# The adaptive norm's first shift and scale made ahead of the other ten, in a two-layer transformer kernel on one Trainium2 core

## The chip, the cores and the metric

The kernel runs on one core of a Trainium2 chip. The metric is the device time in microseconds (us) of one execution. The engines are named as in the profile: PE is the matrix engine (TensorE), PEld its loads of weights, DVE is VectorE, ACT is ScalarE, POOL is GpSimd, SP is SyncE, which here only issues transfers (DMAs). Each engine has a program of its own, runs it in order, and waits on semaphores that other engines and transfers raise.

## What is computed

Two layers act on x (8 sequences, 256 tokens, 128 features). In each, a conditioning vector c gives twelve 128-wide vectors per sequence in all, six a layer, which shift, scale and gate.

```
mod = (silu(c) @ wmod).reshape(8, 6, 1, -1)          # once for each layer, c: 8x128, wmod: 128x768
sa, ca, ga, sb, cb, gb = mod[:, 0], ..., mod[:, 5]
ga, gb = (2*(g >= 0) - 1) * max(abs(g), 0.25)        # for each gate g
h = layernorm(x) * (1 + ca) + sa
x = x + ga * attention(h)                            # layer 0: gated delta rule; layer 1: chunked state space
h = layernorm(x) * (1 + cb) + sb
x = x + gb * ffn(h)                                  # layer 0: 8 experts, top 2; layer 1: butterfly maps
```

The attention of layer 0 projects h to q, k, v and two gates, convolves over four tokens, takes norms, and runs a recurrence over time.

## The kernel before

Features lie on the partitions, tokens along the free axis. The 256 tokens are cut into five windows (32, 32, 64, 64, 64 tokens of each sequence) that pass through the stages of layer 0 behind each other, and into four views of 64 tokens for layer 1. What each engine does, in which order, is written out by hand at the end of its part of `program`, as a list of calls such as `center(("front", 0))` or `project(0, i)`. The function names differ by engine, and the work of one stage is spread over several of them.

The first window's prologue is the part that matters here. SP's `loads` issues the transfers in a fixed order on one queue: x of window 0, the constants C (256 KB), the conditioning vectors `csil` (8 KB), the modulation weights `wm` (768 KB; their space is the upper buffer of `wrep`, by which name the profile knows them), the columns of biases `col` (31.5 KB), the projection matrices M (576 KB), the x of the other windows, then the operands of a fold of the butterfly maps (`wxT` in `ssdb`, `wc`, and a ring of eight 256 KB pieces `hid`), and more. A semaphore rises by 16 for each transfer that has landed.

The layer norm of a window is made in pieces: PE takes the mean away (`center`, psA), ACT squares (`ln_square`), PE averages the squares (`variance`, psB), ACT makes 1/sqrt with a Ln and an Exp (`ln_scale`), DVE multiplies (`ln`, into hf), ACT applies scale and shift, one instruction for each sequence (`modulate`). Then PE projects (`project`) and ACT applies silu to the projections (`projected`).

The modulation: ACT applies silu to both conditioning vectors (`condition`), PE makes twelve products of 128x128 weights with eight columns (`modulation`, psM bank X0, a float32 product being two passes, so 24 passes), DVE copies all to `mod`, adds one to the scales and makes the gates (`modulation`, eight instructions). ACT's `table` loads a new table of functions where the next function isn't in the one held. The silu, the Ln and Exp, and the square root each need a table of their own here.

In the prologue the orders before are: on ACT `ln_square`, `condition`, `ln_scale`, `modulate`, `projected`; on PE `center`, `variance`, `modulation`, `project`, then `fold(0)` and `square_sums(0)` (the sums for the norms of keys and queries); on DVE `biases`, `modulation`, `ln`, `convolve`. On SP the ring's later loads (`fold_load`) wait for folds.

## Time and profile before

| | |
|---|---|
| median of 3 runs | 572.57 us (570.67 to 573.45) |
| the profiled execution | 571.0 us |
| its span, first to last instruction | 568.9 us |
| mean granted TensorE clock | 0.904 of full speed |
| busy: PE, DVE, ACT, POOL | 78%, 66%, 69%, 34% |

The span is what the rows' times count from; 2.1 us of the profiled execution lie outside it. In the timeline's rows the first number is the start, the second the time that the merged instructions cover, "x24" how many there were, and the brackets tell how long the engine was idle before and what ended that. The weight loads (PEld) overlap with the passes (PE).

### The profile page before, as it was taken

To read this page: it belongs to the slowest core of one execution; us is meant where nothing else is said; L and a number is where in the kernel's file an instruction comes from. 1 tells how busy PE (TensorE), PEld (TensorE's weight loads), DVE (VectorE), ACT (ScalarE), POOL (GpSimd) and SP (SyncE) were. 2 spreads that over 40 slices of the span, in tenths; PEclk is the share of its full clock that TensorE was granted. 3 is DMA by queue.
4 is the path that set the end of the run, shared out by engine and by line. 5 is a ranking of instruction groups with operands and counts; after the bars stand their busy time and mean duration, and the time that the engine had idled before them with its cause. 6 is when DMAs were issued, how large, how long until landed. Compare 5 with 4: busy or idle time off the path is not lost.

```text
span 568.9 us, 6438 instructions
## 1 busy us (share of the span) xinstructions
PE 445.5 (78%) x2064; PEld 303.8 (53%) x2064; DVE 376.6 (66%) x663; ACT 392.6 (69%) x661; POOL 193.0 (34%) x188
## 2 busy tenths in 40 slices
PE   5585597479975777998969989999999889864145
PEld 4474573267654654665746656676656566441012
DVE  1326958698979999799998958999231483022800
ACT  3798747757898558689745997746996676924242
POOL 0150961396108971048791104541003000030001
PEclk9988777978999999899988998999999999985557
DMA  7637537232270311800240081000000000000000
GB/s 204 231 122 180 164 100 300 47 93 75 67 140 1 93 40 56 188 0 1 60 109 0 1 189 38 1 1 1 0 1 20 1 1 1 0 18 0 1 1 18
DMA packets 35473, 36.49 MB, mean 64 GB/s; under 512 B 12904, under 2 KB 30832, under 8 KB 35184
## 3 DMA queue, kind: packets, MB, share of 16 engines
q1 hardware_dynamic: 35152, 31.88, 21.2%
q10 hardware_dynamic: 288, 4.19, 1.9%
q8 instruction: 17, 0.28, 0.2%
q14 instruction: 16, 0.13, 0.1%
HBM read 31.61 MB, written 3.28 MB: 61 GB/s over the span
## 4 chain that ended last, share of the span: by engine, by line
PE 34%; DVE 22%; ACT 16%; POOL 11%; issue 9%; DMA 2%; SPq 2%; POOLq 0%; DVEq 0%; ACTq 0%
PE psF L751 8%; PE psS L769 8%; PE psB L708 4%; DVE XX L1798 3%; DVE norm L1795 3%; DVE U L1815 3%; DVE T L1813 3%; DVE T L1817 3%; PE psM L812 3%; ACT L1086 2%; ACT hid L1280 2%; ACT L1088 2%; ACT hS L1129 2%; PE psM L819 2%; POOL G L2154 2%
## 5 line engine op out<-in xcount | busy, mean ns | idle before, releaser
L769 PEld LDWEIGHTS psS<-we2s,hid 128*128 128x128 f32 x1024 | 136.5, 196 | 61.2 <-issue 46.9
L751 PE MATMUL psF<-h,we1s 128*128 128x512 f32 (+1 forms) x320 | 139.7, 528 | 13.2 <-ACT hid L1280 12.5
L769 PE MATMUL psS<-we2s,hid 128*128 128x128 f32 x1024 | 138.9, 280 | 10.8 <-DVE acc L1836 5.5
L1280 ACT ACTIVATE hid<-psF,col 128x512 f32<-128x512 f32 (+1 forms) x160 | 93.2, 598 | 57.6 <-PE psF L751 56.9
L2203 POOL TENSOR_TENSOR QS<-H,qn 128x512 f32<-128x512 f32 x32 | 44.8, 1414 | 95.3 <-DVE H L1823 86.0
L751 PEld LDWEIGHTS psF<-h,we1s 128*128 128x128 f32 x320 | 54.9, 199 | 41.5 <-ACT hid L1280 22.0
L1836 DVE SCALAR_TENSOR_TENSOR acc<-psS,gate,acc 128x128 f32<-128x128 f32 x128 | 36.3, 340 | 33.7 <-PE psS L769 33.7
L1823 DVE TENSOR_TENSOR_SCAN H<-A,T 128x576 f32<-128x576 f32 x32 | 55.3, 1727 | 1.1
L1088 ACT ACT_TABLE_LOAD x41 | 52.6, 1283 | 0.7
L1813 DVE TENSOR_TENSOR T<-wrep,H 128x648 f32<-128x648 f32 x32 | 33.6, 1050 | 14.3 <-DMA wrep<-XX 13.9
L1815 DVE TENSOR_REDUCE U<-T 128x64 f32<-128x576 f32 x32 | 38.7, 1208 | 1.1
L1086 ACT ACT_TABLE_LOAD x30 | 38.5, 1283 | 0.5
L708 PE MATMUL psB<-QS,worep 128*128 128x256 f32 x128 | 32.1, 408 | 7.5 <-POOL QS L2203 7.0
L2225 POOL TENSOR_TENSOR x<-x,brS 128x512 f32<-128x512 f32 x4 | 5.8, 1462 | 93.8 <-DVE brS L1971 93.8
L590 PE MATMUL psA<-x,C 128*128 128x512 f32 (+3 forms) x36 | 21.2, 677 | 16.1 <-DMA C<-consts_dram 6.1
L2186 POOL TENSOR_TENSOR zb<-bg,kn 128x192 f32<-128x192 f32 (+10 forms) x35 | 32.4, 959 | 0.4
L708 PEld LDWEIGHTS psB<-QS,worep 128*128 128x128 f32 x128 | 25.7, 205 | 12.1 <-POOL QS L2203 7.6
L1766 DVE SCALAR_TENSOR_TENSOR zb<-p,col,zb 128x512 f32<-128x512 f32 (+1 forms) x45 | 25.5, 640 | 9.5 <-ACT zb L1184 9.5
L1817 DVE TENSOR_TENSOR T<-krep,U 128x512 f32<-128x512 f32 x32 | 30.7, 959 | 1.1
L2229 POOL TENSOR_TENSOR brS<-brS,mod 128x512 f32<-128x512 f32 x4 | 4.3, 1081 | 77.2 <-ACT brS L1322 77.2
L1106 ACT ACTIVATE sq<-psA 128x512 f32<-128x512 f32 (+3 forms) x18 | 9.8, 544 | 28.3 <-PE psA L590 28.3
L2154 POOL TENSOR_TENSOR G<-G,ag 128x64 f32<-128x64 f32 (+10 forms) x35 | 28.4, 810 | 2.4
(193 smaller groups left out, 734.7 us busy)
## 6 DMA issues: line engine op xcount, KB each, us to landing
wrep<-scratch_dram SPq DMA_DIRECT2D x64, 144.0 KB, 3.6
krep<-scratch_dram SPq DMA_DIRECT2D x64, 128.0 KB, 3.0
hid<-fold_mats_dram SPq DMA_DIRECT2D x22, 256.0 KB, 5.2
we1s<-we_dram ACTq DMA_DIRECT2D x1, 2048.0 KB, 7.9
we2s<-we_dram ACTq DMA_DIRECT2D x1, 2048.0 KB, 12.4
wrep<-XX SPq DMA_DIRECT2D x8, 144.0 KB, 3.4
outT_dram<-x SPq DMA_DIRECT2D x4, 256.0 KB, 2.6
scratch_dram<-XX SPq DMA_DIRECT2D x3, 288.0 KB, 2.1
```

The source lines that it names most:

```text
L708: last = mm(psB[:, at:at + HC], worep[:, e, :], QS[:, e, :], start=(e == 0), stop=(e == DH - 1))
L751: mm(bank[name][:, 0:ncols(w)], we1s[:, e, k * P:(k + 1) * P], h2[w % 2][:, 0:ncols(w)], start=True, stop=True).then_inc(s_hid_mm, 1)
L769: last = mm(bank[name][:, t * P:(t + 1) * P], hid[n % 2][:, k, t * P:(t + 1) * P], we2s[:, e, k, :], start=(k == 0), stop=(k == HT - 1))
L1086: nc.scalar.preload_act_table_set(LN_EXP)
L1088: nc.scalar.preload_act_table(kind)
L1280: nc.scalar.activation(hid[x_ % 2][:, k, 0:c], psF[n % 2][:, 0:c], ACT.Silu, bias=pc("be1", HT * e + k)).then_inc(s_hid_done, 1)
L1813: v_.tensor_tensor(T9[:, :, :, :], wv, prev.unsqueeze(3).broadcast_to([P, DH + 1, NB, C9]), ALU.mult).then_inc(s_prod_done, 1)
L1815: v_.tensor_reduce(U[:, :, :], T9[:, :, :, 1:].rearrange("p e b i -> p b i e"), AX.X, ALU.add).then_inc(s_u_delta, 1)
L1817: v_.tensor_tensor(T9[:, 0:DH, :, 1:], kv, U[:, :, :].unsqueeze(1).broadcast_to([P, DH, NB, CH]), ALU.mult).then_inc(s_outer_done, 1)
L1823: v_.tensor_tensor_scan(H[g % NH_][:, 0:DH, :, :].rearrange("p e b i -> p (e b i)"), A9[g % NA][:, :, :, :].rearrange("p e b i -> p (e b i)"),
L2154: g_.tensor_tensor(Gw(n, j)[:, :, 1:], Gw(n, j + 1), a[:, :, j + 1:j + 2].broadcast_to([P, bc, CH - 1 - j]), ALU.mult).then_inc(s_g_done, 1)
L2203: g_.tensor_tensor(o, H[g % NH_][:, 0:DH, :, 1:], q, ALU.mult).then_inc(s_qs_done, 1)
```

## The change

The modulation's first shift and first scale, which the norm of the first windows needs, are made by two products of their own, ahead of PE's `variance`; DVE copies them (adding one to the scale) ahead of `ln`. The other ten products follow behind the variance, into bank X1, and DVE's rest of the modulation follows behind `ln`. ACT's `condition` becomes its first operation. The modulation weights come in three transfers: the first two products' (128 KB), then, behind M, the rest of layer 0's (256 KB) and layer 1's (384 KB); the columns move ahead of them. The conditioning and the columns now raise one semaphore, and M and the last two parts of the weights raise one.

PE's first rows. psA is the centered x, psB the mean of squares, `psM<-csil,wrep` a modulation product and `psS<-hf,M` a projection. Before:

```order
L590 MATMUL psA<-x,C 128x264 [waits const_in,x_in0]
L599 MATMUL psB<-sq,C 128x264 [waits ln_sq]
L606 MATMUL psM<-csil,wrep 128x8 [waits csil_done]
L606 MATMUL psM<-csil,wrep 128x8 x11
L621 MATMUL psS<-hf,M 128x264 [waits ln_h,mat_in]
L621 MATMUL psS<-hf,M 128x264
L621 MATMUL psF<-hf,M 128x264
```

After:

```order
L592 MATMUL psA<-x,C 128x264 [waits const_in,x_in0]
L608 MATMUL psM<-csil,wrep 128x8 [waits mod_in,csil_done]
L608 MATMUL psM<-csil,wrep 128x8
L601 MATMUL psB<-sq,C 128x264 [waits ln_sq]
L616 MATMUL psM<-csil,wrep 128x8 [waits mat_in]
L616 MATMUL psM<-csil,wrep 128x8 x9
L630 MATMUL psS<-hf,M 128x264 [waits ln_h,mat_in]
L630 MATMUL psS<-hf,M 128x264
L630 MATMUL psF<-hf,M 128x264
```

Two of the twelve products now stand ahead of the variance, and ten between it and the projections, behind a wait for M's semaphore, which now counts three transfers.

ACT's first rows; `csil<-csil` is the silu of the conditioning, `sq` the squares and then 1/sqrt, `hf<-hf,mod` the modulation of h. Before:

```order
L1106 ACT_TABLE_LOAD
L1106 ACTIVATE sq<-psA 128x264 [waits ln_c]
L1088 ACT_TABLE_LOAD
L1093 ACTIVATE csil<-csil 128x16 [waits mod_in]
L1086 ACT_TABLE_LOAD
L1116 ACTIVATE sq<-psB,eps 128x264 [waits ln_v,eps_set]
L1118 ACTIVATE sq<-sq 128x264 [waits ln_log]
L1129 ACTIVATE hf<-hf,mod 128x33 [waits mod_scale,mod_done,ln_n1]
```

After:

```order
L1098 ACT_TABLE_LOAD
L1103 ACTIVATE csil<-csil 128x16 [waits col_in]
L1116 ACTIVATE sq<-psA 128x264 [waits ln_c]
L1096 ACT_TABLE_LOAD
L1126 ACTIVATE sq<-psB,eps 128x264 [waits ln_v,eps_set]
L1128 ACTIVATE sq<-sq 128x264 [waits ln_log]
L1141 ACTIVATE hf<-hf,mod 128x33 [waits mod_scale,ln_n1]
```

The silu moved ahead of the square, waits for `col_in` where it waited for `mod_in`, and one table load of three is gone.

DVE's rows behind its memsets; `hf<-psA,sq` is the normalization, rows with `mod`, `gsg` and `gab` are the modulation's. Before:

```order
L1699 TENSOR_SCALAR hab<-col 128x2 [waits col_in,set]
L1700 TENSOR_TENSOR dbias<-col 128x1
L1724 COPY mod<-psM 128x96 [waits mod_mm]
L1728 TENSOR_SCALAR mod<-mod 128x4x8 [waits mod_read]
L1729 TENSOR_SCALAR gsg<-mod 128x32
L1730 TENSOR_SCALAR gab<-mod 128x32
L1732 TENSOR_TENSOR gab<-gab,mod 128x32 [waits mod_neg]
L1734 TENSOR_SCALAR gsg<-gsg 128x32 [waits mod_sign]
L1736 TENSOR_SCALAR gab<-gab 128x32 [waits mod_abs]
L1739 TENSOR_TENSOR mod<-gsg,gab 128x4x8 [waits mod_abs,mod_sign]
L1720 TENSOR_TENSOR hf<-psA,sq 128x8x33 [waits ln_sd]
L1766 SCALAR_TENSOR_TENSOR zb<-p,col,zb 128x256 [waits tap0] x3
```

After:

```order
L1711 TENSOR_SCALAR hab<-col 128x2 [waits col_in,set]
L1712 TENSOR_TENSOR dbias<-col 128x1
L1736 COPY mod<-psM 128x8 [waits mod_mm]
L1737 TENSOR_SCALAR mod<-psM 128x8
L1732 TENSOR_TENSOR hf<-psA,sq 128x8x33 [waits ln_sd]
L1741 COPY mod<-psM 128x80 [waits mod_mm]
L1745 TENSOR_SCALAR mod<-mod 128x3x8 [waits mod_read]
L1746 TENSOR_SCALAR gsg<-mod 128x32
L1747 TENSOR_SCALAR gab<-mod 128x32
L1749 TENSOR_TENSOR gab<-gab,mod 128x32 [waits mod_neg]
L1751 TENSOR_SCALAR gsg<-gsg 128x32 [waits mod_sign]
L1753 TENSOR_SCALAR gab<-gab 128x32 [waits mod_abs]
```

Two small instructions stand ahead of the normalization where eight stood, and eight follow it.

```diff
--- before.py
+++ after.py
@@ -475,10 +475,12 @@
                     off += NB * (b - a)
                     if n == 0:
                         sp.dma_start(C[:, :, :], consts).then_inc(s_const_in, 16)
-                        sp.dma_start(csil[:, :, :], cT).then_inc(s_mod_in, 16)
-                        sp.dma_start(wm[:, :, :], wmod).then_inc(s_mod_in, 16)
+                        sp.dma_start(csil[:, :, :], cT).then_inc(s_col_in, 16)
                         sp.dma_start(col[:, :], cols).then_inc(s_col_in, 16)
+                        sp.dma_start(wm[:, 0, 0:2 * P], wmod[:, 0, 0:2 * P]).then_inc(s_mod_in, 16)
                         sp.dma_start(M[:, :, :], mats).then_inc(s_mat_in, 16)
+                        sp.dma_start(wm[:, 0, 2 * P:], wmod[:, 0, 2 * P:]).then_inc(s_mat_in, 16)
+                        sp.dma_start(wm[:, 1, :], wmod[:, 1, :]).then_inc(s_mat_in, 16)
                 sp.dma_start(wxT[:, :, :], w_exp).then_inc(s_fold_in, 16)
                 sp.dma_start(wc[:, :, :], w_con).then_inc(s_fold_in, 16)
                 for j in range(RING):
@@ -518,7 +520,7 @@
                     if h > 1:
                         sp.wait_ge(s_prod_done, CPH * (h - 1))
                     elif h == 1:
-                        sp.wait_ge(s_mod_mm, 1)
+                        sp.wait_ge(s_mod_mm, 2)
                     for d in range(DH):
                         sp.dma_start(wrep[h % 2][d::DH, 0:DH, :], scratch[w, 1, :, i * H9:(i + 1) * H9].rearrange(
                             "(h e) n -> h e n", e=DH)).then_inc(s_wrep_in[h % 2], 16)
@@ -599,21 +601,28 @@
                 mm(psB[:, 0:k], cst("mean"), sq[:, 0:k], start=True, stop=True).then_inc(s_ln_v, 1)
                 read["B"] = s_ln_log, n + 1
 
+            def first_modulation():
+                pe.wait_ge(s_csil_done, 1)
+                pe.wait_ge(s_mod_in, 16)
+                for i in range(2):
+                    last = mm(X0[:, i * NB:(i + 1) * NB], wm[:, 0, i * P:(i + 1) * P], csil[:, 0, :], start=True, stop=True)
+                last.then_inc(s_mod_mm, 1)
+                read["X0"] = s_mod_scale, 2
+
             def modulation():
-                pe.wait_ge(s_csil_done, 1)
-                for l in range(2):
-                    for i in range(6):
-                        last = mm(X0[:, (6 * l + i) * NB:(6 * l + i + 1) * NB], wm[:, l, i * P:(i + 1) * P],
-                                  csil[:, l, :], start=True, stop=True)
+                pe.wait_ge(s_mat_in, 48)
+                for j in range(2, 12):
+                    l, i = j // 6, j % 6
+                    last = mm(X1[:, j * NB:(j + 1) * NB], wm[:, l, i * P:(i + 1) * P], csil[:, l, :], start=True, stop=True)
                 last.then_inc(s_mod_mm, 1)
-                read["X0"] = s_mod_read, 1
+                read["X1"] = s_mod_read, 1
 
             def project(n, i):
 
                 name = proj_banks(n)[i]
                 if i == 0:
                     if n == 0:
-                        pe.wait_ge(s_mat_in, 16)
+                        pe.wait_ge(s_mat_in, 48)
                     pe.wait_ge(s_ln_h, LN["front", n] + 1)
                 free(name)
                 if i < 3:
@@ -821,6 +830,7 @@
                 read["X0"] = s_ffn_read, v + 1
 
             center(("front", 0))
+            first_modulation()
             variance(("front", 0))
             modulation()
             for i in range(0, 5):
@@ -1089,7 +1099,7 @@
 
             def condition():
                 table(ACT.Silu)
-                act.wait_ge(s_mod_in, 32)
+                act.wait_ge(s_col_in, 32)
                 nc.scalar.activation(csil[:, :, :], csil[:, :, :], ACT.Silu).then_inc(s_csil_done, 1)
 
             def load_weights():
@@ -1123,8 +1133,10 @@
                 _, out, _, (s, c, l) = ln_tile(key)
                 act.wait_ge(s_ln_n1, n + 1)
                 if n == 0:
+                    act.wait_ge(s_mod_scale, 2)
+                if n == 1:
                     act.wait_ge(s_mod_done, 1)
-                    act.wait_ge(s_mod_scale, 1)
+                    act.wait_ge(s_mod_scale, 3)
                 for b in range(NB):
                     last = nc.scalar.activation(out[:, b, :], out[:, b, :], ACT.Identity, bias=mod[:, 6 * l + s, b:b + 1],
                                                 scale=mod[:, 6 * l + c, b:b + 1])
@@ -1141,7 +1153,7 @@
                 ps = bank[proj_banks(n)[i]]
                 table(ACT.Silu)
                 if n == 0 and i == 0:
-                    act.wait_ge(s_col_in, 16)
+                    act.wait_ge(s_col_in, 32)
                 if i < 3:
                     k = b - a
                     act.wait_ge(s_proj_mm, 5 * n + i + 1)
@@ -1321,8 +1333,8 @@
                 act.wait_ge(s_x3_done, v + 1)
                 nc.scalar.activation(brS[:, :], X0, ACT.Identity, bias=dbias[:, 0:1]).then_inc(s_ffn_read, 1)
 
+            condition()
             ln_square(("front", 0))
-            condition()
             ln_scale(("front", 0))
             modulate(("front", 0))
             for i in range(0, 3):
@@ -1695,7 +1707,7 @@
                 dve.wait_ge(s_set, 16)
 
             def biases():
-                dve.wait_ge(s_col_in, 16)
+                dve.wait_ge(s_col_in, 32)
                 v_.tensor_scalar(hab[:, :], col[:, COL["ba"]:COL["ba"] + 2], 0.5, None, ALU.mult).then_inc(s_half_done, 1)
                 v_.tensor_tensor(dbias[:, :], pc("bcon"), pc("downb"), ALU.add).then_inc(s_ub_done, 1)
 
@@ -1719,11 +1731,16 @@
                     dve.wait_ge(s_dec_mm, i + 1)
                 v_.tensor_tensor(out, bt(psA[:, 0:k]), bt(rs[:, 0:k]), ALU.mult).then_inc(s_ln_n1, 1)
 
+            def first_modulation():
+                dve.wait_ge(s_mod_mm, 1)
+                v_.tensor_copy(mod[:, SA, :], X0[:, SA * NB:(SA + 1) * NB]).then_inc(s_mod_scale, 1)
+                v_.tensor_scalar(mod[:, CA, :], X0[:, CA * NB:(CA + 1) * NB], 1.0, None, ALU.add).then_inc(s_mod_scale, 1)
+
             def modulation():
-                dve.wait_ge(s_mod_mm, 1)
-                v_.tensor_copy(mod[:, :, :], X0[:, 0:12 * NB].rearrange("p (i b) -> p i b", b=NB)).then_inc(s_mod_read, 1)
+                dve.wait_ge(s_mod_mm, 2)
+                v_.tensor_copy(mod[:, 2:12, :], X1[:, 2 * NB:12 * NB].rearrange("p (i b) -> p i b", b=NB)).then_inc(s_mod_read, 1)
                 dve.wait_ge(s_mod_read, 1)
-                scale = mod[:, 1:12:3, :]
+                scale = mod[:, 4:12:3, :]
                 gates = mod[:, 2:12:3, :]
                 v_.tensor_scalar(scale, scale, 1.0, None, ALU.add).then_inc(s_mod_scale, 1)
                 v_.tensor_scalar(gsg[:, :, :], gates, 0.0, 2.0, ALU.is_ge, ALU.mult).then_inc(s_mod_sign, 1)
@@ -1972,8 +1989,9 @@
 
             begin()
             biases()
+            first_modulation()
+            ln(("front", 0))
             modulation()
-            ln(("front", 0))
             convolve(0)
             carry_hf(1)
             carry(1)
```

## Rows read from the trace of the kernel before

**Rows 1.** The page, part 4: the chain's shares of the span by engine.

```profile
PE 34%; DVE 22%; ACT 16%; POOL 11%; issue 9%; DMA 2%; SPq 2%; POOLq 0%; DVEq 0%; ACTq 0%
```

**Rows 2.** Chain that ended last, 0 to 80 us: start us, us, what.

```profile
19.07 2.10 PE psS L621 x4
...
28.41 1.43 PE psS L636 x4
```

**Rows 3.** Timeline, 0 to 45 us: start us, us, engine, line, operation, tiles, count.

```profile
6.06 1.22 PE L590 MATMUL psA<-x,C 128*128 128x264 f32 x2 [6.06 <-DMA C<-consts_dram]
7.32 0.39 ACT L1106 ACTIVATE sq<-psA 128x264 f32<-128x264 f32 x1 [5.31 <-PE psA L590]
7.73 1.28 ACT L1088 ACT_TABLE_LOAD   x1
...
7.76 1.25 PE L599 MATMUL psB<-sq,C 128*128 128x264 f32 x2 [0.48 <-ACT sq L1106]
...
9.02 0.22 ACT L1093 ACTIVATE csil<-csil 128x16 f32<-128x16 f32 x1
...
9.29 5.19 PEld L606 LDWEIGHTS psM<-csil,wrep 128*128 128x128 f32 x24 [1.03 <-ACT csil L1093]
...
10.55 0.48 ACT L1116 ACTIVATE sq<-psB,eps 128x264 f32<-128x264 f32 x1
11.06 0.42 ACT L1118 ACTIVATE sq<-sq 128x264 f32<-128x264 f32 x1
...
14.61 0.26 DVE L1724 COPY mod<-psM 128x96 f32<-128x96 f32 x1 [6.16 <-PE psM L606]
...
15.91 0.42 DVE L1720 TENSOR_TENSOR hf<-psA,sq 128x264 f32<-128x264 f32 x1
...
16.37 2.55 ACT L1129 ACTIVATE hf<-hf,mod 128x33 f32<-128x33 f32 x8 [4.89 <-DVE hf L1720]
...
20.38 0.48 ACT L1155 ACTIVATE p<-psS,col 128x264 f32<-128x264 f32 x1 [0.15 <-issue]
...
22.73 1.08 PEld L671 LDWEIGHTS psM<-ssdb,hid 128*128 128x128 f32 x8
```

**Rows 4.** Timeline of SP's DMA issues, 0 to 26 us: start, time of issuing.

```profile
1.83 0.42 SPq L478 DMA_DIRECT2D csil<-cT_dram  x1
2.30 0.43 SPq L479 DMA_DIRECT2D wrep<-wmod_dram  x1
2.77 0.44 SPq L480 DMA_DIRECT2D col<-cols_dram  x1
3.26 0.43 SPq L481 DMA_DIRECT2D M<-mats_dram  x1
3.73 6.23 SPq L474 DMA_DIRECT2D x<-xT_dram  x4
...
11.72 4.54 SPq L485 DMA_DIRECT2D hid<-fold_mats_dram  x8
```

**Rows 5.** DMA issues, 0 to 30 us and 12.5 to 13: size, us to landing.

```profile
wrep<-wmod_dram SPq DMA_DIRECT2D x1, 768.0 KB, 5.6
M<-mats_dram SPq DMA_DIRECT2D x1, 576.0 KB, 6.3
...
col<-cols_dram SPq DMA_DIRECT2D x1, 31.5 KB, 5.3
csil<-cT_dram SPq DMA_DIRECT2D x1, 8.0 KB, 4.3
...
hid<-fold_mats_dram SPq DMA_DIRECT2D x2, 256.0 KB, 6.3
```

**Rows 6.** Page part 2 (granted clock), and tile M, 0 to 30 us: min/median/max ns.

```profile
PEclk9988777978999999899988998999999999985557
...
L621 PE MATMUL psS<-hf,M x4: 647/647/780, 19.1 to 20.5; 128*128 128x264 f32 x4
...
L627 PE MATMUL psS<-hf,M x4: 382/392/607, 21.8 to 22.7; 128*128 128x256 f32 x4
```

## The prediction

> **What bounds the kernel now.** I read the page's chain first. No engine fills it: TensorE (PE) has 34%, VectorE (DVE) 22%, ScalarE (ACT) 16% [rows 1]. So this is one long chain of hand-overs between engines whose order is written out by hand, and time taken out of any link of the chain is worth its full length as long as nothing else arrives later. Next I read the chain's early pieces: the projections of the first window at 19.07 us and the square sums at 28.41 us are in it [rows 2]. Everything ahead of 19.07 is therefore prologue that the whole kernel waits for, and the change is made there.
>
> The timeline of the first 23 us shows what that prologue waits for [rows 3]. The reader should follow four things in it.
> - PE centers x from 6.06 to 7.28, ACT squares it (7.32), PE sums the squares (7.76 to 9.01).
> - ACT loads the silu table in the middle of this (7.73, 1.28 us) and applies silu to the conditioning (9.02 to 9.24). After it ACT has to load the table for Ln and Exp, another 1.28 us, so Ln starts at 10.55 although its sums were there at 9.01. Exp ends at 11.48.
> - PE starts the modulation products only after the silu: 24 passes (12 products, two passes each) in 5.19 us, that is 0.216 us a pass, with results at 14.6.
> - DVE has the modulation's eight small instructions ahead of the normalization in its program. It sits idle for 6.16 us until the copy at 14.61 and normalizes at 15.91, 4.4 us after Exp has ended. ACT's modulation of h (eight instructions, 2.55 us) then runs from 16.37 to 18.92, and the projections begin.
>
> So the wait that ends last is the one for the twelve products, through DVE's order. The weights are no part of it: they landed at 2.30 + 5.6 = 7.9 us [rows 4, 5].
>
> **The change, part by part, with its times.** I rebuild the prologue link by link.
>
> Silu first. ACT loads the silu table while nothing has arrived and then waits for two transfers, the conditioning and the small columns tile. The conditioning landed at 1.83 + 4.3 = 6.1, and 8 KB behind the 256 KB of constants (there at 6.06) cost under 0.1 us [rows 3, 4, 5]. The columns landed at 2.77 + 5.3 = 8.1, but behind the 768 KB of weights; now they stand ahead of them. I take 6.5 (upper bound 8.1), so silu ends near 6.8, before the square at 7.32, which is queued behind it on ACT and stays where it is. One table load of 1.28 us disappears, and the load for Ln takes 7.73 to 9.01.
>
> Two products ahead of the variance. The first 128 KB of weights need one sixth of the bytes that were there at 7.9, so they are in by 7.28. Four passes at 0.216 us take PE from 7.28 to 8.15. The variance, ready at 7.71, moves to 8.2 to 9.45. Ln follows at 9.5 (10.55 before), Exp ends at 10.4.
>
> DVE's order. The normalization stands behind only the two small copies now (less than the 0.26 us of the big copy each, over by 8.7). It runs 10.4 to 10.85. ACT modulates from 10.9 to 13.45 and loads the silu table until 14.75. DVE does the other modulation work (from 14.61 on before) after this, under ACT's and PE's work; nothing needs it before the fold and the second window.
>
> Ten products. They stand ahead of the projections in PE's queue and wait for M and for all weights, three transfers. Before, M landed at 3.26 + 6.3 = 9.6 with all the weights ahead of it [rows 4, 5], so the bytes up to there are the same. Lower bound 9.6, upper bound 10.5 (two more issues of 0.47 us each on SP's queue, the step from 2.30 to 2.77); I take 10.0, as the bytes and not the issues filled that stretch. Twenty passes at 0.216 us plus the hand-over end at 14.4. **This, not h (ready at 13.45), is now what the projections wait for.** They begin at 14.45 instead of 19.07, a gain of **4.6 us**; ACT's first projected activation, 1.3 us behind that start (19.07 to 20.38), comes at 15.75, later than its table at 14.75. With the weights at 9.6 the gain is 5.0, at 10.5 it is 4.1. With the columns as late as 8.1 everything from the square on slips by about 1 us, the ten products start near 10.45 and the gain is also 4.1.
>
> The Trainium skill (DMA: Bandwidth & Descriptors, "Anatomy of one DMA") gives each transfer a fixed cost of about 2.0 us; paid one after another, two more transfers would put the ten products 4 us later and leave a gain of some 0.6 us. The rows speak against paying it in series: the 8 KB transfer issued at 1.83 landed under 0.1 us behind its predecessor.
>
> What SP pushes back. Two more issues stand ahead of the four x loads, the fold's operands and the ring, about 1 us. The ring's eight issues take 4.54 us from 11.72 on, so the third begins near 12.9 and landed about 12.9 + 6.3 = 19.2 [rows 4, 5] and can now come as late as 20.2. PE's fold begins at 22.73 - 4.6 = 18.1 instead of 22.73, so it will meet pieces that are not there yet: before it had some 3 us of cover, now it can wait up to 1 us for each half of fold 0. The fold's eight first passes took 1.08 us [rows 3], so its sixteen others take about 2.1, and with the last piece at 20.2 they end at 22.3. Behind it in PE's queue are the square sums, due at 28.41 - 4.6 = 23.8. So 1.5 us of slack hide this, and I cost it at nothing; if the ring came 2.5 us later than before, each further microsecond would cost one. The waits are on fixed thresholds of transfers and products; those behind the first window (the ring's later loads, the spread of keys, the experts' weights) are issued after compute that moves with the chain, so they move too.
>
> **Sum.** 571.0 us for the profiled execution less 4.6 gives 566.4. It stood 1.6 us under the median of 572.57, so the predicted median is 572.57 - 4.6 = **568.0 us**, 0.8% less.
>
> **TensorE's clock.** The clock line of the page shows 9 tenths or more for the first two slices (28 us), then 8, 8, 7, 7, 7; but the projection passes up to 21.4 us took 647 ns for 264 columns, and those from 21.8 on mostly 382 to 392 for 256 [rows 6]. By the passes, then, PE runs at the lower of its two levels (1.2 GHz) up to about 21 us and at 2.4 after. It had been almost without a gap from 6.06 to 14.6 and did not speed up, then idle until 19.07, and 2.4 us of projections later it was fast. I assume the same: 8-column products don't raise it, the projections do.
>
> **The rivals.**
> A. The clock rises earlier. PE now has no idle stretch between 7.3 and the projections. If the unbroken work counted, the six projection passes would take 0.38 instead of about 0.6 us, some 1 us more gained: 572.57 - 5.6 = 567.0. Against it: the gapless products of before stayed slow. The Trainium skill (TensorE: Matmul & The Clock Gate, "What's actually happening") has sustained activity release the throttle; by that rule A is what comes, but the 5.19 us of products at an unchanged 0.216 us a pass disagree with it. Chance 0.12.
> B. The loads come late. The last weights, or the ring, arrive about 2 to 3 us later than I have them, because split transfers pay in series or share the engines with x. Then 2 to 2.5 us remain: 570.3. For it: SP's x loads took 6.2 us for four issues [rows 4], so that queue is full. Against: total bytes are unchanged. Chance 0.12.
> C. The edit does its work but the end doesn't move with it. Something behind the first window, a DMA or an engine's own backlog, holds the chain where it was, or TensorE's low-clock stretches fall otherwise: 572.0. For it: PE carries 34% of the chain and its clock changes by stretches [rows 6]. Against: I find no wait after 23 us on something with a fixed time. Chance 0.12.
> D. Slower than before. The place is PE's share of the chain, 0.34 x 568.9 = 193 us. Each microsecond of it that moves from full to half clock costs 0.5. Since an earlier start shifts every busy and idle stretch against whatever decides the clock, the low stretches can lengthen; the mean clock was 0.904, so (1 - 0.904) / 0.5 = 19% of the span, 109 us, were at half. From 9.2 us more of them on the chain the gain is gone, from 15 us on the kernel is slower by 0.5%: 575.5 us. For it: the clock line already swings between 7 and 9 tenths in the first half [rows 6]. Against: uniform shifting leaves the gaps' lengths alone. Chance 0.05.
>
> **How the numbers follow.** My forecast has 0.59. The three runs before lie within 2.8 us (570.67 to 573.45), so 0.5% (2.9 us) is about what a measurement of this kernel can tell from no change. The forecast's own bounds 4.1 to 5.0 give 567.6 to 568.5, and A reaches down to 567; with run scatter of 1.4 us the low end is 565.7. The high end takes in B: 571.0. C and D (0.17) and a little of A's edge stay outside. Faster by over 0.5%: forecast, A and a part of B, 0.78. Within 0.5%: the rest of B and C, 0.17. Slower: 0.05.
>
> **What the changed profile would show.** Right: one table load and the silu before the square, which stays at 7.3; Ln near 9.5; no DVE wait between Exp and the normalization at 10.4; PE's ten products from about 10.0 to 14.4 and the projections directly behind them without a gap; the square sums near 23.8; the first ring load after the prologue near 20 us. Wrong: products that wait past 10.5 for a transfer, a square later than 7.4, a PE wait for ring pieces that ends after 22 us, or a prologue that is 4.6 us shorter while the first chunk of the recurrence starts less than 4 us earlier. The last would point to C.

## The result and the profile after

The changed kernel took 564.69 us (median of 6 runs, 562.6 to 566.26) against 571.65 (median of 6, 568.14 to 576.19) for the kernel before: a ratio of 0.9882, 95% interval 0.9848 to 0.9916. That is 7.0 us less between the medians, 4.8 to 8.7 by the interval. (The ratio is not the quotient of the two medians, which is 0.9878.) The ratios and intervals of this document leave out executions more than 1.5% above the fastest of their kernel, of which these twelve have none, while medians and ranges are over all. The forecast was faster, as it came, but by 4.6 us, and the 564.69 us lie 1.0 us below the range's low end of 565.7.

The page of the changed kernel first: its span, the granted clock and the chain's shares. Before these were 568.9 us and [rows 1, 6].

```profile
span 563.6 us, 6444 instructions
...
PEclk9988697889988988999989998999999999985557
...
PE 35%; DVE 23%; ACT 16%; POOL 11%; issue 9%; DMA 3%; SPq 2%; POOLq 0%; DVEq 0%; ACTq 0%
```

The shares are within one point of what they were, and the span of this execution is 5.3 us shorter. In the timeline of the changed kernel (start, us, engine, line, operation) the links of the prologue stand as follows; they answer to [rows 3].

```profile
5.47 1.22 PE L592 MATMUL psA<-x,C 128*128 128x264 f32 x2 [5.47 <-DMA C<-consts_dram]
5.76 0.21 ACT L1103 ACTIVATE csil<-csil 128x16 f32<-128x16 f32 x1 [3.75 <-DMA col<-cols_dram]
...
6.48 0.86 PE L608 MATMUL psM<-csil,wrep 128*128 128x8 f32 x4
6.72 0.39 ACT L1116 ACTIVATE sq<-psA 128x264 f32<-128x264 f32 x1 [0.75 <-PE psA L592]
7.13 1.28 ACT L1096 ACT_TABLE_LOAD   x1
...
7.19 1.23 PE L601 MATMUL psB<-sq,C 128*128 128x264 f32 x2
...
8.52 0.48 ACT L1126 ACTIVATE sq<-psB,eps 128x264 f32<-128x264 f32 x1
9.03 0.42 ACT L1128 ACTIVATE sq<-sq 128x264 f32<-128x264 f32 x1
9.49 0.43 DVE L1732 TENSOR_TENSOR hf<-psA,sq 128x264 f32<-128x264 f32 x1 [1.87 <-ACT sq L1128]
9.96 2.55 ACT L1141 ACTIVATE hf<-hf,mod 128x33 f32<-128x33 f32 x8 [0.50 <-DVE hf L1732]
...
10.76 4.44 PE L616 MATMUL psM<-csil,wrep 128*128 128x8 f32 x20 [2.34 <-DMA wrep<-wmod_dram]
...
15.04 2.11 PE L630 MATMUL psS<-hf,M 128*128 128x264 f32 x4
...
16.36 0.48 ACT L1167 ACTIVATE p<-psS,col 128x264 f32<-128x264 f32 x1 [2.55 <-issue]
...
19.11 1.84 PEld L680 LDWEIGHTS psM<-ssdb,hid 128*128 128x128 f32 x8
...
24.39 1.13 PE L645 MATMUL psS<-norm,C 128*128 128x256 f32 x4 [1.46 <-ACT norm L1208]
```

Link by link against [rows 3]: the silu is over by 5.97, the square begins at 6.72 (7.32), Ln at 8.52 (10.55), the normalization at 9.49 (15.91), h is ready at 12.51 (18.92). Then PE is late: the ten products begin at 10.76 and end at 15.2, the projections follow, and the first projected activation begins at 16.36 (20.38). The lead here is 4.0 us. The chain of waits names the reason (start, us, what):

```profile
4.19 6.52 DMA wrep<-wmod_dram
...
10.76 4.44 PE psM L616 x20
15.19 1.96 PE psS L630 x4
...
24.35 1.28 ACT L1098
```

The chain now begins in the transfers. The last 384 KB of weights, issued at 4.19, hold PE up to 10.76; after that come the ten products and the projections. The DMA issues of the same trace (size, us to landing), which answer to [rows 5]:

```profile
wrep<-wmod_dram SPq DMA_DIRECT2D x1, 384.0 KB, 6.5
...
C<-consts_dram SPq DMA_DIRECT2D x1, 256.0 KB, 4.1
...
col<-cols_dram SPq DMA_DIRECT2D x1, 31.5 KB, 3.4
csil<-cT_dram SPq DMA_DIRECT2D x1, 8.0 KB, 3.6
```

The columns, ahead of the big transfer, landed in 3.4 us instead of 5.3. The constants and the conditioning, issued at the same times as before, landed 0.6 and 0.7 us sooner (the constants in 4.1 instead of 4.7, the conditioning in 3.6 instead of 4.3, [rows 5]).

The lead of 4.0 us did not stay 4.0. Read at the recurrence's scans it was 2.2 at the first, 6.3 at the fifth, 7.5 at the ninth, 5.3 at the last. So something behind the prologue, in code that the change leaves alone, moved the time by more than the forecast's whole error of 3.3 us. The prediction had named one of these readings as a sign of being wrong: the first chunk of the recurrence less than 4 us earlier. It came, for the first triangular solve (the start of the first chunk) began at 38.69 against 40.82, 2.1 us earlier (3.0 in the second trace below), but the end did not fall short as rival C had it.

### The profile page after: what moved, and what is told of

The parts are those of the page before. It is cut to its first block, busy times and chain, and to the rows that moved or that the text cites. A ratio compares the mean times of both kernels' runs of the same rounds, so it can differ in the third digit from the quotient of the medians.

```text
span 563.6 us, 6444 instructions
## 1 busy us (share of the span) xinstructions
PE 449.8 (80%) x2064; PEld 308.5 (55%) x2064; DVE 378.2 (67%) x665; ACT 391.9 (70%) x660; POOL 193.0 (34%) x188
## 3 DMA queue, kind: packets, MB, share of 16 engines
q10 hardware_dynamic: 288, 4.19, 1.9%
## 4 chain that ended last, share of the span: by engine, by line
PE 35%; DVE 23%; ACT 16%; POOL 11%; issue 9%; DMA 3%; SPq 2%; POOLq 0%; DVEq 0%; ACTq 0%
PE psF L760 8%; PE psS L778 8%; PE psB L717 4%; DVE XX L1815 3%; DVE norm L1812 3%; DVE U L1832 3%; DVE T L1830 3%; ACT L1098 3%; DVE T L1834 3%; PE psM L821 3%; ACT L1096 3%; ACT hid L1292 2%; ACT hS L1141 2%; PE psM L828 2%; POOL G L2172 2%
## 5 line engine op out<-in xcount | busy, mean ns | idle before, releaser
L760 PE MATMUL psF<-h,we1s 128*128 128x512 f32 (+1 forms) x320 | 141.2, 533 | 14.7 <-ACT hid L1292 13.1
L2221 POOL TENSOR_TENSOR QS<-H,qn 128x512 f32<-128x512 f32 x32 | 46.9, 1483 | 94.1 <-DVE H L1840 84.9
L717 PE MATMUL psB<-QS,worep 128*128 128x256 f32 x128 | 34.2, 428 | 8.2 <-POOL QS L2221 7.6
L717 PEld LDWEIGHTS psB<-QS,worep 128*128 128x128 f32 x128 | 27.1, 216 | 13.5 <-POOL QS L2221 8.4
L592 PE MATMUL psA<-x,C 128*128 128x512 f32 (+3 forms) x36 | 19.8, 636 | 15.9 <-DMA C<-consts_dram 5.5
L1732 DVE TENSOR_TENSOR hS<-psA,sq 128x512 f32<-128x512 f32 x8 | 5.5, 683 | 34.7 <-ACT sq L1128 34.7
L2172 POOL TENSOR_TENSOR G<-G,ag 128x64 f32<-128x64 f32 (+10 forms) x35 | 27.2, 777 | 2.4
## 6 DMA issues: line engine op xcount, KB each, us to landing
we2s<-we_dram ACTq DMA_DIRECT2D x1, 2048.0 KB, 12.5
```

What stands on the lines that cost most here:

```text
L717: last = mm(psB[:, at:at + HC], worep[:, e, :], QS[:, e, :], start=(e == 0), stop=(e == DH - 1))
L760: mm(bank[name][:, 0:ncols(w)], we1s[:, e, k * P:(k + 1) * P], h2[w % 2][:, 0:ncols(w)], start=True, stop=True).then_inc(s_hid_mm, 1)
L2172: g_.tensor_tensor(Gw(n, j)[:, :, 1:], Gw(n, j + 1), a[:, :, j + 1:j + 2].broadcast_to([P, bc, CH - 1 - j]), ALU.mult).then_inc(s_g_done, 1)
L2221: g_.tensor_tensor(o, H[g % NH_][:, 0:DH, :, 1:], q, ALU.mult).then_inc(s_qs_done, 1)
```

## The experiments

All were timed in five rounds beside the kernel before; an interval is the 95% interval of the ratio. "Lead" is the start of the first projected activation before (20.38) less the same in the variant's trace. Comments in the cuts of code below are this document's, and "..." marks what is left out.

**The two kernels again.** `before_again` and `after_again` are the two kernels unchanged.

> The kernel before, unchanged, taken as if it were a variant. It shows how far two series of one program differ. Theory S (the median moved by the 4.0 us of the prologue, the rest is scatter from where TensorE's low-clock stretches fall): a ratio of 0.997 to 1.003, single runs spread over 5 us or more, and in its trace the low-clock stretches at other places than in the first trace of this same program, with stage times up to 240 us that differ by 1 to 3 us. Theory W (the low stretches stand fixed against the program, and the change moves them to a better place for good): the low stretches of this trace lie where those of the first did, to 1 us.

> The changed kernel, unchanged, a second series. S: the ratio falls back towards 1 - 4.0/571.6 = 0.993 (0.991 to 0.995), and the lead over the kernel before, read from stage to stage, changes at other places than between the first two traces. W: 0.988 again (0.986 to 0.990), with the same jumps of the lead.

Measured: before_again 572.34 us, ratio 1.0018 (0.9994 to 1.0042), single runs 570.36 to 576.99; after_again 565.54 us, ratio 0.9906 (0.987 to 0.9941). The lead of after_again was 4.8 us, since its last weights landed earlier and the ten products began at 9.96. Here is one group of PE instructions, the sixteen passes of the fold's last step (matmuls into psM), in four traces. First the timeline of the kernel before:

```profile
73.33 3.62 PE L674 MATMUL psM<-hid,ssdb 128*128 128x128 f32 x16
```

Its windows, 70 to 80 us (us, PE, PEld, DVE, ACT, POOL busy, then the granted clock, DMA share, GB/s):

```profile
70.00:80.00 10.00, 7.68 (x45) 7.45 (x46) 6.90 (x8) 1.28 (x3) 10.00 (x11) 0.66 0.34 90
```

The timeline of the kernel before, second trace:

```profile
74.64 3.62 PE L674 MATMUL psM<-hid,ssdb 128*128 128x128 f32 x16
```

Its windows:

```profile
70.00:80.00 10.00, 6.38 (x34) 6.20 (x34) 8.17 (x9) 0.62 (x2) 9.78 (x12) 0.66 0.38 106
```

The timeline of the changed kernel:

```profile
68.62 1.95 PE L683 MATMUL psM<-hid,ssdb 128*128 128x128 f32 x16
```

Its windows, with a granted clock of 1.00:

```profile
70.00:80.00 10.00, 9.24 (x52) 6.92 (x51) 8.99 (x16) 7.08 (x14) 7.88 (x8) 1.00 0.53 172
```

The timeline of the changed kernel, second trace:

```profile
68.22 3.62 PE L683 MATMUL psM<-hid,ssdb 128*128 128x128 f32 x16
```

Its windows, with a granted clock of 0.50:

```profile
70.00:80.00 10.00, 10.00 (x38) 8.44 (x38) 5.62 (x8) 2.39 (x5) 6.98 (x7) 0.50 0.14 37
```

The same program took 1.95 us for these passes in one execution and 3.62 in the next; the granted clock of the stretch was 1.00 (2.4 GHz) in the one and 0.50 (1.2 GHz) in the other. Start times of the recurrence's scans, from the four timelines, in us:

| | before | before_again | after | after_again |
|---|---|---|---|---|
| first projected activation | 20.38 | 20.35 | 16.36 | 15.56 |
| scan 1 | 60.58 | 61.88 | 58.40 | 57.53 |
| scan 5 | 106.67 | 108.17 | 100.33 | 105.98 |
| scan 9 | 163.45 | 165.03 | 155.96 | 163.15 |
| last scan | 357.29 | 359.48 | 351.99 | 357.39 |

The two traces of the changed kernel are 0.9 us apart at scan 1 and 5.65 at scan 5. Theory S was right that one program's traces differ by microseconds, and that after_again would fall nearer to 1, though the interval of 0.9906 holds both 0.988 (W) and 0.993 (S). W in its strict form, the same jumps in each trace of a program, is false for the changed kernel. In the two traces of before the stretches at 50 to 110 us did lie alike: the granted clock of each 10 us there differs by at most 0.13 between them.

**DVE's order undone** (`dve_old`).

```diff
             first_modulation()
-            ln(("front", 0))
             modulation()
+            ln(("front", 0))
             convolve(0)
```

> The changed kernel with one part undone: DVE makes the whole rest of the modulation ahead of the normalization again, so this waits for the ten products. They end at 14.4 to 15.2 (weights landed at 10.0 to 10.7 in the two traces of the changed kernel), DVE's copy and seven more instructions end 1.3 us later, the normalization near 16.3, h near 19.3 and the first projected activation near 20.7, where the kernel before has 20.4. If DVE's order is what carries the lead, the lead at this activation is -0.5 to +0.3 us, although silu, two products and the split are all in. Rival (the earlier silu and the earlier Ln carry it): the lead stays over 1 us.

Measured: normalization at 16.10, first projected activation at 20.56, a lead of -0.2 us; 570.15 us, ratio 0.9964 (0.9933 to 0.9995). Without DVE's order there is no lead: silu, two early products and the split are all in and give nothing alone. This shows that the order is needed, not that it is enough. No run has the order alone, without the two products made ahead of the others, and ACT needs their shift and scale before it can modulate h. Unexpected was that the kernel without a lead was still 0.4% faster.

**The silu back in the middle** (`silu_mid`).

```diff
-            condition()
             ln_square(("front", 0))
+            condition()
             ln_scale(("front", 0))
```

> The changed kernel with the silu behind the first square on ACT again, as in the kernel before. The third table load is back, the silu comes near 8.6, the two products end at 9.5, and the variance behind them in PE's queue at 10.7 (8.4 in the changed kernel); Ln at 10.8, h ready near 14.8, the ten products 10.8 to 15.2, the projections at 15.2, where the changed kernel has 14.25 to 15.04. Theory (the ten products bound it): 0.2 to 1.0 us of the lead are lost, the lead at the first projected activation is 3.3 to 4.2 us. Rival (the silu's place carries its full 2.3 us): lead near 2.3 us.

Measured: normalization at 12.02, ten products from 10.74, projections at 15.19, lead 3.9 us; 566.22 us, ratio 0.9927 (0.9887 to 0.9967). Its h came 2.5 us later than in the changed kernel and cost only 0.1 to 0.9 us of lead, because the projections wait for the ten products too, and these ended at 15.0. They themselves began late, at 10.74, behind the later variance, where their weights had landed at 10.2 (4.19 + 6.0). As the changed kernel stands, most of the 2.5 us that ACT's reordering saves is slack.

**One transfer for the weights** (`one_transfer`).

```diff
-  sp.dma_start(wm[:, 0, 0:2 * P], wmod[:, 0, 0:2 * P]).then_inc(s_mod_in, 16)
+  sp.dma_start(wm[:, :, :], wmod).then_inc(s_mod_in, 16)
   sp.dma_start(M[:, :, :], mats).then_inc(s_mat_in, 16)
-  sp.dma_start(wm[:, 0, 2 * P:], wmod[:, 0, 2 * P:]).then_inc(s_mat_in, 16)
-  sp.dma_start(wm[:, 1, :], wmod[:, 1, :]).then_inc(s_mat_in, 16)
...
-                pe.wait_ge(s_mat_in, 48)      # ten products: no wait
-                        pe.wait_ge(s_mat_in, 48)
+                        pe.wait_ge(s_mat_in, 16)
```

> The changed kernel with all modulation weights in one transfer, behind the columns and ahead of M, all twelve products waiting for it alone. First products at about 8.0 instead of 6.5, variance behind them to 10.2, Ln at 10.3 (8.5), h ready near 14.3 (12.5), but the ten products need no transfer any more and run 10.2 to 14.6, the projections start at 14.7, where the changed kernel has 14.25 to 15.04. Theory (the last transfer, landed at 10.0 to 10.7, bounds the split version): within 0.5 us of the changed kernel either way. Rival (the split itself carries gain because the first products come early): 1.5 us or more later at the first projected activation.

Measured: first products at 7.85, normalization at 10.99, ten products from 9.71 to 14.0, projections at 14.15 after PE had idled 0.17 us for h, lead 4.9 us; 563.35 us, ratio 0.9875 (0.9832 to 0.9917). The split gives no lead over the changed kernel's 4.0 and 4.8. Here h and the ten products end together, and without the split PE never waits for a late last part.

**The ten products out of the projections' way** (`ten_late`).

```diff
             variance(("front", 0))
-            modulation()
             for i in range(0, 5):
                 project(0, i)
...
             center(("front", 1))
-            fold(1)
+            fold_up(1)
+            modulation()          # into bank F1, waits for the late transfers
+            fold_down(1)
```

and DVE's `modulation()` behind `carry(1)`, the projections' wait for M alone, the wait for the gates at the third window's `modulate`.

> The ten products leave the projections' way: PE makes them inside the fold's second step, where it idled 2.9 us at 27 us, into another bank; the projections wait for M alone, the rest of the weights for nothing in the prologue, and DVE's eight modulation instructions follow the first convolution. If the ten products and their last transfer (landed at 10.7) are what bounds the prologue of the changed kernel, the projections start at 12.6 behind h instead of at 15.0, and the first projected activation comes at 13.9 instead of 16.4: another 2.4 us, ratio to the kernel before 0.984 to 0.989 by S (4.0 + 2.4 = 6.4 us) and 0.984 by W (7.0 + 2.4). Rival: fold 0's ring pieces are then what PE waits for (they come at about 20 us), it holds up the square sums, and under 1 us is gained over the changed kernel.

Measured: projections at 12.75, lead 6.3 us; 564.83 us, ratio 0.9846 (0.9804 to 0.9889), runs from 558.46 to 570.06. The products are what bounds the changed kernel's prologue. PE did wait 1.3 us for the first ring piece at 17.96, as the rival said, but the square sums were not held up: the lead was 6.5 at the norms. It was 6.1 at the start of the first triangular solve and 4.6 at the first scan; where those 1.5 us went was not followed up. The end did not follow the lead either: the median is level with the changed kernel's 564.69 and 565.54.

**ACT held back** (`hold4`).

```diff
             modulate(("front", 0))
+            table(ACT.Silu)
+            act.wait_ge(s_const_in, 16)
+            for i in range(11):            # 128x512 copies of the constants into tiles not yet in use
+                nc.scalar.activation(hold[i], C..., ACT.Copy)
             for i in range(0, 3):
                 projected(0, i)
```

> The changed kernel with eleven copies (128x512, some 0.6 us each) on ACT between its table load at 12.5 to 13.8 and the first projected activation, so that this comes at about 20.3 us as in the kernel before. If all of the gain is the prologue's lead: ratio 0.998 to 1.002. If something else of the change helps by itself (the transfers, the DVE order, a better place of the clock's stretches): the ratio stays below 0.997, by W near 0.995.

Measured: lead 0.75 us at the first projected activation but 1.9 at the norms, since PE had made three projections meanwhile; 567.08 us, ratio 0.9919 (0.9892 to 0.9946). The expectation was missed, in part by the hold's design, but 1.9 us of lead still came with 4.6 us of gain between the medians. Together with dve_old this asked what gives about 2 us besides the lead.

**Products before the projections to raise the clock** (`warm`).

```diff
+            warm(3, ("F0", "F1"))          # 128x256 products of constants
             center(("front", 0))
             first_modulation()
             variance(("front", 0))
+            warm(1, ("F0",))
             modulation()
```

> The changed kernel with three extra products of 128x256 on constants ahead of the centering (PE idle from 2.9 to 5.5 us) and one between the variance and the ten products (idle 1.5 to 2.3 us). It leaves nothing out. Rival A of the prediction (unbroken work raises PE's clock before the projections): the ten products take about 2.4 us instead of 4.4, the projections start at 13 and the first projected activation comes 2 us earlier than in the changed kernel. If narrow products don't raise the clock and the extra ones are too few: the ten products stay at 4.4 us, the projections' start stays within 0.5 us, and the centering may even be held up by up to 0.8 us.

The timeline of this kernel:

```profile
2.97 2.93 PE L623 MATMUL psF<-segm 128*128 128x256 f32 x6 [2.97 <-DVE segb L1713]
...
10.61 2.80 PE L616 MATMUL psM<-csil,wrep 128*128 128x8 f32 x20 [1.35 <-DMA wrep<-wmod_dram]
...
13.27 2.11 PE L635 MATMUL psS<-hf,M 128*128 128x264 f32 x4
...
14.58 0.48 ACT L1174 ACTIVATE p<-psS,col 128x264 f32<-128x264 f32 x1 [0.68 <-issue]
```

The ten products took 2.80 us instead of 4.44, although they began at nearly the same time as in the changed kernel (10.61). But the projections behind them were at the slow pace again (four passes in 2.11 us, as in [rows 2] and in the trace after). Three windows of this kernel show the fall (start and end, length, PE, PEld, DVE, ACT, POOL busy, then the granted clock, DMA share, GB/s):

```profile
10.60:11.60 1.00, 0.99 (x9) 0.99 (x9) 0.00 (x0) 1.00 (x5) 0.00 (x0) 1.00 0.55 105
12.60:12.80 0.20, 0.20 (x2) 0.20 (x3) 0.00 (x0) 0.18 (x2) 0.00 (x0) 0.50 0.47 92
13.40:15.40 2.00, 2.00 (x6) 1.59 (x6) 1.19 (x8) 0.99 (x2) 0.00 (x0) 0.50 0.96 256
```

The granted clock fell from 1.00 to 0.50 at about 12.5 us, during the narrow products, after wide products up to 9.26 and 1.35 us without work. The same column reads 1.00 in the prologue of the changed kernel, although its projections have the pace that warm has at 0.50:

```profile
15.40:18.00 2.60, 2.60 (x7) 1.98 (x7) 1.01 (x8) 0.96 (x2) 0.00 (x0) 1.00 1.05 399
```

So ahead of the first change on record the column can't be trusted in these traces, and the pace of the passes decides, as the prediction took it [rows 6]. Lead 5.8 us; 565.51 us, ratio 0.9865 (0.9822 to 0.9908). Rival A's faster products came behind wide products, where the narrow ones by themselves had stayed slow, and its faster projections did not come. In the Trainium skill (TensorE: Matmul & The Clock Gate, "What's actually happening") sustained activity releases the throttle; the fast products behind the wide ones agree with this, the 24 back-to-back passes of the kernel before, at 0.216 us each to their end, do not.

**PE fed in its gaps.** `fed_before`, `fed_after`, `fed_dve_old`, `fed_hold4` and `fed_ten` are the kernels above with extra products of constants where PE idled between 23 and 115 us.

```diff
+            def feed(k, name="F1"):
+                free(name)
+                for _ in range(k):
+                    mm(bank[name][:, 0:512], cst("mean"), C[:, :, :].rearrange("p a n -> p (a n)"), start=True, stop=True)
...
             fold(0)
+            feed(1)
             square_sums(0)
...
             variance(("front", 2))
+            feed(7)
             square_sums(1)
             fold(6)
             fold(7)
+            feed(2)
```

and 2 inside fold 1, 3 around the first router norms, 4 ahead of the first gate rows.

> The kernel before with extra products of constants (128x512, results never read) in PE's idle gaps between 23 and 115 us: 1 behind fold 0, 2 inside fold 1, 7 ahead of the second window's square sums, 2 behind fold 7, 3 around the first router norms, 4 ahead of the gate rows. It leaves nothing out. If the low-clock stretches follow PE's idle gaps, those up to 115 us vanish or shrink, the time falls by 3 to 8 us and the runs scatter less. If they don't follow, the time rises by what the extra products cost, 0 to 4 us.

> The changed kernel with the same extra products in the same gaps. With the low stretches up to 115 us out of both, what is left between this and the fed kernel before is the prologue's lead: theory S says 4.0 to 4.8 us less than the fed kernel before, at every stage from the first projected activation to the end. Theory W (the change puts the clock's low stretches to a better place, worth 2 us more) says the difference to the fed kernel before shrinks to the lead while the difference between the unfed ones stays at 5.5 to 7. Rival E (something else behind the prologue gives 2 us): 6 to 7 us between the fed ones too.

> The changed kernel with DVE's old order and the extra products in PE's gaps. Without feeding, this order had no lead at the first projected activation (-0.2 us) and was still 0.4% faster than the kernel before. Theory W (that 0.4% is where the low-clock stretches fall): fed, it is the fed kernel before to 1 us, ratio to the kernel before 0.992 to 0.996. Theory E (the split, the silu or the order of transfers gives something behind the prologue that no stage of the trace shows): 2 us below the fed kernel before, ratio 0.988 to 0.991.

> The version with the ten products inside fold 1 together with the extra products (those in fold 1 left out, since the ten products stand there). Lead at the first projected activation 6.3 us as in the unfed version; by theory S it is 1.5 us below the fed changed kernel and 6.3 below the fed kernel before: 561.2 us, ratio 0.980 to 0.983, the fastest of all. Rival: the lead of 6.3 is partly given back at the first scan (4.6 left in the unfed trace), then it is level with the fed changed kernel, 0.985.

The pair was then repeated on another chip, with the held version beside it.

> The fed kernel before once more: 567 to 569 us, ratio to the kernel before 0.992 to 0.996. It is the base for the two others of this set.

> The fed changed kernel once more. W: 4.0 to 5.5 us below fed_before2 (its lead is 4.8). E: 6 to 7 us below.

> The changed kernel with eleven copies on ACT ahead of the first projected activation and the extra products in PE's gaps; lead at the norms 1.9 us. W: 1 to 3 us below fed_before2. E: 4 to 5 us below, as unfed.

Measured medians and ratios to the kernel before: fed_before 567.47 (0.9938, 0.9912 to 0.9964) and 568.1 (0.9947, 0.9914 to 0.9981); fed_after 562.85 (0.985, 0.9817 to 0.9883) and 562.55 (0.9851, 0.9792 to 0.9909); fed_dve_old 568.28 (0.9966, 0.9933 to 0.9999); fed_hold4 566.97 (0.9939, 0.99 to 0.9977); fed_ten 561.78 (0.9832, 0.9787 to 0.9878).

Against the kernels that were fed and timed beside them, fed_after was 4.6 and 5.6 us below fed_before (between the medians of each pair), and fed_hold4 1.1 us. For the second pair and fed_hold4, W had asked for 4.0 to 5.5 and 1 to 3, E for 6 to 7 and 4 to 5. The interval of fed_dve_old excludes E's 0.988 to 0.991, while its 0.9966 lies just above W's 0.992 to 0.996, and fed_ten came within 0.6 us of its 561.2.

The means over single runs set the gains beside the leads, with 95% bounds (1.96 standard errors, from the runs' scatter). Unfed gains are against the 108 runs of before that all these series gave, fed ones against the 24 of the two fed_before. "Ratios' runs" are those that the ratios count (99 and 22 of the two bases). The lead at the norms is that of the unfed trace, read where ACT copies the square sums (29.86 in the kernel before, 29.64 in before_again, against which each lead is 0.2 less).

| variant | lead at the norms | gain unfed, all runs | unfed, ratios' runs | gain fed, all runs | fed, ratios' runs |
|---|---|---|---|---|---|
| dve_old | 0.0 | 1.6 ± 1.5 | 1.7 ± 1.4 | 0.5 ± 1.4 | 0.0 ± 1.3 |
| hold4 | 1.9 | 4.2 ± 1.3 | 3.8 ± 1.3 | 2.1 ± 1.6 | 1.6 ± 1.4 |
| silu_mid | 4.1 | 5.3 ± 1.5 | 4.9 ± 1.5 | | |
| the changed kernel | 4.2 and 5.0 | 6.1 ± 1.4 | 5.7 ± 1.3 | 5.0 ± 1.9 | 5.0 ± 1.5 |
| one_transfer | 5.0 | 7.0 ± 2.3 | 6.6 ± 2.3 | | |
| warm | 6.0 | 5.7 ± 2.2 | 7.9 ± 2.2 | | |
| ten_late | 6.5 | 6.6 ± 3.2 | 8.2 ± 3.2 | 7.3 ± 1.8 | 6.8 ± 1.7 |

Fed, each gain is the lead within 1 us. Unfed, over all runs, the first five lie 1.2 to 2.3 us above it, warm and ten_late do not; over the ratios' runs all seven do, by 0.8 to 1.9. That fits W: the surplus goes when PE's gaps are filled in both kernels. No single row settles it, since the bounds are as wide as the surplus.

Three readings speak against taking W as shown. First, more full clock is not what the changed kernel has: the mean granted clock is 0.902 over its 12 executions and 0.901 over the 102 of the kernel before that have one on record, and 0.898 for dve_old with its gain of 1.6. (Between executions of the kernel before, 0.01 of clock goes with 1.9 us, so 1.5 us would take 0.008.) Of W only the place of the low stretches is left as a cause, and no run shows that one directly. Second, feeding did not raise the clock alike in both. From 23 to 115 us the granted clock was 0.83 and 0.84 in the two traces of before, 0.94 and 0.98 in those of fed_before, but 0.85 and 0.79 in the changed kernel and 0.92 and 0.91 in fed_after. So the surplus may also go because the extra products fit the gaps of the kernel before better, a rival that no run tests. Third, the lead did not hold "at every stage" as fed_after's expectation said. Between the two pairs of fed traces it was 4.7 and 4.9 us at the first projected activation, 4.8 and 2.5 at the first scan and 0.8 and 0.6 at the fifth; both profiled executions of fed_after were the slowest of their six.

Feeding by itself took 4.4 and 4.1 us off the kernel before by the medians, 2.8 ± 1.1 by the means of all runs, and did not make the runs scatter less (563.97 to 575.68); that part of its expectation failed.

## Why the prediction was wrong

**What failed** is the last step, how the numbers follow: "with run scatter of 1.4 us the low end is 565.7". The scatter was taken from three runs, and the clock was allowed to act only against the forecast (C and D, both slower) or in the prologue (A). And where the clock's low stretches fall behind 23 us was priced at nothing in the sum. The runs showed single executions of the kernel before from 564.81 to 576.99 (standard deviation 2.5 us over the 108, where 1.4 was taken), and two traces of the changed kernel 5.65 us apart at scan 5, one of them with a granted clock of 0.50 where the other had 1.00. Over the 102 executions of before with a clock on record, a mean granted clock higher by 0.01 goes with 1.9 us less, with a correlation of only -0.5, so the clock is part of the scatter and not shown to be all of it.

Most of the miss is the base. The forecast subtracted from 572.57, the median of three runs; the six beside the changed kernel gave 571.65, 0.9 us less, and the result missed the low end by 1.0. Read as a gain, the low end was 6.9 us, the measured gain 7.0, and the repeat's 6.1. That the result fell just outside the range and not just inside is luck; that the range was too narrow for this scatter is not.

**The size.** The prologue was priced at 4.6 us and measured 4.0 and 4.8 in the two traces. The rest of the 7.0 (6.1 in the repeat; 6.1 ± 1.4 over all runs), 1 to 3 us, arose behind the prologue. The fed kernels speak against a second gain from the change itself: fed, DVE's old order gave 0.5 ± 1.4. That the place of the low-clock stretches gave it is argued, not shown, and whether it is a lasting advantage of the changed kernel or luck of some runs is open.

**The links.**
- Silu near 6.8, square unmoved at 7.3: the order was right, the times early. Columns landed at 2.29 + 3.4 = 5.7 (6.5 taken), and the constants half a microsecond sooner, so the centering began at 5.47.
- Two products ahead of the variance were to cost it 0.45 us. They cost under 0.1: the variance began at 7.19, 0.08 behind the square's end at 7.11, where it had been 0.05 before. The centering had come earlier, so they ran beside the square from 6.48 on.
- Normalization at 9.49 (10.4), h at 12.51 (13.45). Both right in mechanism, 0.9 us early by the two points above.
- Ten products from 10.0, bounds 9.6 and 10.5: 10.76 and 9.96. The last part took 6.5 and 5.7 us to land. With 10.76 in this trace and 10.61 in warm the upper bound was too near, and the prediction's sign "products that wait past 10.5 for a transfer" came. This link, and not h, is the one that the projections waited for, as forecast, and so the 0.9 us of the links ahead were worth nothing. One_transfer and ten_late confirm it from two sides.
- The projections at 14.45: 15.04 and 14.25. Square sums at 23.8: 24.39 and 23.59. PE never waited for the ring's pieces in the changed kernel: its fold's first weight loads began at 19.11 and 18.31, where the prediction had 18.1. The first load into the ring behind these came at 21.17 and 19.76, near the 20 named.
- The fixed cost of transfers in series: the weights' last part came 0.3 to 1.1 us behind where all of them and M had landed before (9.6), not 4. The section of the Trainium skill that the prediction names gives the 2.0 us for transfers that GpSimd issues; these are SP's, and no run here measures the fixed part of one.

**The rivals.** A didn't come in the changed kernel, whose ten products stayed at 4.44 us; in warm, behind wide products, they took 2.80. B: the last weights were late by 0.2 us beyond the bound in one trace, not by 2 to 3. C's second half, low stretches that fall otherwise, did come between the traces (0.50 against 1.00 from 70 to 80 us), but not its end of 572.0. D didn't come; every series of the changed kernel is faster.

## What to carry to other kernels

When a wait is removed, look for the order that held it: here the lead hung on one swap on a third engine (DVE), behind two products made ahead of the rest, while the earlier silu met mostly slack and the split transfers gave nothing. Price a front-end gain by the link that is late next (here ten products behind a transfer), then take that link out of the way too: moved into a gap of PE's, it was worth another 1.5 to 2.3 us of lead, with which the medians of the fed kernels fell by 0.8 to 1.1 us and their means by 2.3 ± 2.2, the medians of the unfed not at all. Where the matrix engine's clock moves between two levels in a kernel, take the range for the total from many runs, since a lead of 4.8 us after the prologue was 0.3 at the ninth scan of one trace, and one of 4.0 was 7.5 in another. And subtract a forecast from as many runs of the kernel before as the result will be compared with: three runs put this one 0.9 us off. The lowest median here was fed_ten's, 561.78 us.

## What the runs showed of the hardware that was not expected

- Where the 768 KB transfer was issued right behind the conditioning, the constants and the conditioning, issued ahead of it, landed later: 4.6 to 4.8 and 4.2 to 4.4 us (before, before_again and the two fed_before) against 4.1 to 4.3 and 3.5 to 3.6 in every variant in which the 31.5 KB of columns stood between. One_transfer, which keeps the 768 KB in one piece, has 4.3 and 3.6.
- Narrow products of eight columns, twenty passes back to back, took 4.44 us in the changed kernel and 2.80 in warm, behind wide products; the granted clock fell to 0.50 during them and stayed there for the projections.
- PE's sixteen passes of one step took 1.95 or 3.62 us in two executions of one program, with a granted clock of 1.00 and 0.50 from 70 to 80 us.
- The granted clock read 1.00 from the start of the traces up to its first recorded change, also where the passes had the slow pace (four projection passes in 2.11 us at 1.00 in the changed kernel, at 0.50 in warm).
